# Three of eight comparisons of each head on GpSimd in the first layer of a two-layer graph attention kernel

## What is computed

```
s_src, s_dst = per node and head          # Wh . a_src, Wh . a_dst
e = s_src[:, None, :] + s_dst[None, :, :]
e = where(e >= 0, e, 0.2 * e)             # leaky relu
e = where(adj > 0, e, -9e15)
attention = softmax(e, axis=1)
h' = einsum('ijh,jhd->ihd', attention, Wh)
x1 = layernorm(x + elu(h'))
```

## Time and profile before

| what | value |
|---|---|
| median of three runs | 916.73 us (915.87 to 918.69) |
| the profiled execution | 914.89 us |
| its span, first to last instruction | 913.1 us |
| busy share of the span: PE, DVE, ACT, POOL | 92%, 83%, 76%, 5% |
| mean granted TensorE clock | 0.976 of full speed |
| chunk 0 (units with XORs from 85.5), chunks 1, 2, 3 | to 175.75, then 120.78, 119.18, 128.17 us |
| all after chunk 3 | 369.2 us |

### The profile page before, as it was taken

How to read it: one execution, slowest core, us unless ns; L and a number is a source line. 1 busy time by engine, 2 the same in 40 slices (tenths; PEclk the granted TensorE clock), 3 DMA queues, 4 the chain that set the end, 5 groups by cost and what they waited for, 6 DMA issues and landing times.

```text
span 913.1 us, 24394 instructions
## 1 busy us (share of the span) xinstructions
PE 839.0 (92%) x10868; PEld 686.8 (75%) x10868; DVE 761.4 (83%) x1306; ACT 694.4 (76%) x815; POOL 43.0 (5%) x80
## 2 busy tenths in 40 slices
PE   8496999989999889999998898599999999999995
PEld 6496999978999879999998884355555555555552
DVE  3978889899988999889997889775877786878876
ACT  3999998897999989999986994968373654637222
POOL 3200000000000000000000000000000100000000
PEclk9799999999999999999999999799999999999998
DMA  8999377703658227113040002430324453644000
GB/s 146 177 106 249 54 86 77 233 25 35 85 71 197 84 25 86 34 69 143 25 118 19 7 27 68 70 104 13 104 86 159 137 177 104 198 129 153 2 12 14
DMA packets 42065, 84.67 MB, mean 93 GB/s; under 512 B 6242, under 2 KB 31332, under 8 KB 41316
## 3 DMA queue, kind: packets, MB, share of 16 engines
q0 software_dynamic: 12416, 33.56, 26.3%
q1 hardware_dynamic: 29540, 49.50, 15.1%
HBM read 112.27 MB, written 21.12 MB: 146 GB/s over the span
## 4 chain that ended last, share of the span: by engine, by line
PE 50%; ACT 24%; DVE 18%; issue 3%; DMA 3%; POOL 1%; SPq 0%; DVEq 0%; ACTq 0%
PE bank L1299 21%; PE bank L688 18%; ACT ring L620 16%; PE bank L1277 7%; ACT masks L767 3%; DVE ring L653 3%; DVE ring L633 3%; DMA adj_tiles<-in_adj_dram 3%; PE bank L1289 2%; PE bank L536 2%; ACT masks L523 1%; DVE evac L704 1%; DVE ring L657 1%; DVE ring L663 1%; ACT moving L573 1%
## 5 line engine op out<-in xcount | busy, mean ns | idle before, releaser
L688 PE MATMUL bank<-moving,ring 128*128 128x99 bf16 (+1 forms) x6528 | 451.9, 218 | 12.2 <-DVE ring L663 8.8
L688 PEld LDWEIGHTS bank<-moving,ring 128*128 128x128 fp8e4 x6528 | 388.2, 98 | 14.3 <-DVE ring L663 10.0
L620 ACT ACTIVATE ring<-s_rows,scores 128x1024 fp8e4<-128x1024 f32 x372 | 393.1, 1141 | 4.4 <-PE bank L688 3.7
L688 PE MATMUL bank<-moving,masks 128*128 128x99 bf16 x1664 | 222.7, 209 | 18.3 <-DVE evac L704 14.7
L688 PEld LDWEIGHTS bank<-moving,masks 128*128 128x128 fp8e4 x1664 | 163.1, 98 | 20.3 <-DVE ring L657 9.1
L1299 PE MATMUL bank<-moving,masks 128*128 128x387 bf16 x1056 | 178.2, 327 | 0.0
L767 ACT ACTIVATE masks<-s_rows,adj_tiles 128x512 fp8e4<-128x512 f32 x256 | 157.8, 709 | 0.1
L1299 PEld LDWEIGHTS bank<-moving,masks 128*128 128x128 fp8e4 x1056 | 101.7, 96 | 73.0
L653 DVE SCALAR_TENSOR_TENSOR ring<-ring,masks 128x1024 int32<-128x1024 int32 x93 | 113.1, 1217 | 10.9 <-ACT ring L620 10.8
L663 DVE TENSOR_TENSOR ring<-masks,ring 128x1024 int32<-128x1024 int32 x76 | 93.1, 1225 | 26.9 <-PE bank L688 25.2
L395 ACT ACTIVATE ring<-ring 128x4 f32<-128x4 f32 (+1 forms) x24 | 4.9, 205 | 141.0 <-DVE ring L311 115.3
(11 more groups left out here) (214 smaller groups left out, 630.7 us busy)
## 6 DMA issues: line engine op xcount, KB each, us to landing
masks_kept<-masks SPq DMA_DIRECT2D x4, 4096.0 KB, 17.2
masks<-masks_kept SPq DMA_DIRECT2D x8, 2048.0 KB, 9.9
adj_tiles<-in_adj_dram POOLq DMA_DIRECT2D x24, 512.0 KB, 8.5
s_rows<-score_rows SPq DMA_DIRECT2D x14, 512.0 KB, 4.8
ring<-masks_kept POOLq DMA_DIRECT2D x11, 512.0 KB, 3.9
first_part<-masks_kept POOLq DMA_DIRECT2D x11, 512.0 KB, 3.8
second_part<-masks_kept POOLq DMA_DIRECT2D x10, 512.0 KB, 4.0
adj_tiles<-in_adj_dram POOLq DMA_DIRECT2D x16, 256.0 KB, 14.1
```

The lines of the kernel that those rows point to most:

```text
L620: last = act.activation(j_tile(below, k), s_rows[:, h % 2, :], ACT.Sign, bias=scores[:, g * JU + k, h:h + 1], saturate=False)
L688: last = pe.matmul(bank[b][:, at + lo:at + hi], mask, moving[:, j, h, lo:hi], start=first, stop=(j == T - 1), skip_group_check=True)
```

## The change

- `COMPARES` replaces `ON_ACT`, with three letters. In chunks 1 to 3 each head is `APAAPAPA`: ScalarE five units, GpSimd (P) three, VectorE none. Chunk 0 stays as it was.
- GpSimd's comparison (`pool_unit`) is four tensor_scalar instructions per unit, from f32 scores, (score + score) x -1e20, written as a byte. VectorE's AND for such a unit has a constant besides, which keeps one bit of each byte.
- The direct units of chunks 1 to 3 are 4, 4 and 8, where they were 8, 8 and 19.
- The XOR is a scalar_tensor_tensor instruction with a logical shift by zero ahead of it, where it was a tensor_tensor instruction, in all chunks.
- GpSimd's transfers of adjacency rows now stand between its comparisons, each behind unit u for the groups that TensorE turns at unit u - 4.
- SP's loads of score rows also wait for GpSimd.

```diff
-    ON_ACT = [who == "A" for who in
-              "VAVAAVAA" "AVAVAAVA" "AVAVAAVA" "AVAVAAVA"
-              "AVAAVAAA" "AVAAVAAA" "AVAAVAAA" "AVAAVAAA"
...
+    COMPARES = ("VAVAAVAA" "AVAVAAVA" "AVAVAAVA" "AVAVAAVA"
+                "APAAPAPA" "APAAPAPA" "APAAPAPA" "APAAPAPA"
...
-              "DD------" "DD------" "DD------" "DD------"
-              "DD------" "DD------" "DD------" "DD------"
-              "DD-DD-D-" "DD-DD-D-" "DD-DD-D-" "DD-D-D--"]
+              "D-------" "D-------" "D-------" "D-------"
+              "D-------" "D-------" "D-------" "D-------"
+              "D--D----" "D--D----" "D--D----" "D--D----"]
...
+        def pool_unit(pool, c, u):
+
+            h, g = divmod(u, UH)
+            if g == 0:
+                wait_s(pool, c, u)
+            if ON_POOL[c * U + u]:
+                wait_slot(pool, c, u)
+                below = below_slot(c, u).bitcast(U8)
+                for k in range(JU):
+                    last = pool.tensor_scalar(j_tile(below, k), s_rows[:, h % 2, :], scores[:, g * JU + k, h:h + 1],
+                                              FAR, ALU.add, ALU.mult)
+                last.then_inc(pool_compared, 1)
+            if g == UH - 1:
+                pool.wait_ge(pool_compared, pool_count(c, u + 1))
+                pool.sem_inc(s_read_pool, 1)
...
+            elif ON_POOL[c * U + u]:
+                dve.wait_ge(pool_compared, pool_count(c, u + 1))
+                dve.scalar_tensor_tensor(out=below, in0=below, scalar=TWO * 0x01010101, in1=m, op0=ALU.bitwise_and,
+                                         op1=ALU.bitwise_and).then_inc(done, 1)
...
-                dve.tensor_tensor(above_slot(c, u).bitcast(I32), m, below, ALU.bitwise_xor).then_inc(unit_ready, 1)
+                dve.scalar_tensor_tensor(out=above_slot(c, u).bitcast(I32), in0=below, scalar=0, in1=m,
+                                         op0=ALU.logical_shift_right, op1=ALU.bitwise_xor).then_inc(unit_ready, 1)
...
+                    if before > H:
+                        sp.wait_ge(s_read_pool, before - H)
...
                 for c in range(1, NC):
-                    for t in range(CT):
...
-                        load_adj(pool, c, t)
+                    for u in range(U):
+                        pool_unit(pool, c, u)
+                        for q in groups_at(c, u - POOL_AHEAD):
+                            t = q // QT
+                            if q % QT == QT - 1 and t + AHEAD < CT:
+                                load_next(c + 1, t + AHEAD)
+                            elif q % QT == QT - 1 and c + 2 < NC:
+                                load_next(c + 2, t + AHEAD - CT)
```

34 lines of the change are left out of this document (24 added, 10 removed).

## The result

| | before | after |
|---|---|---|
| median on the chip | 916.3 us (914.98 to 918.69) | 945.59 us (945.06 to 946.5) |
| span of the profiled execution | 913.1 us | 943.3 us |
| mean granted TensorE clock | 0.976 | 0.958 |
| chunks 1, 2, 3 | 120.78, 119.18, 128.17 us | 129.22, 129.45, 139.97 us |
| all after chunk 3 | 369.2 us | 367.9 us |

A forecast was written before the change was run, and what follows sets the result against it. PE, VectorE and ScalarE were taken as close together, VectorE setting head 0, PE and ScalarE holding each other in head 2. Terms -10.3 - 8.7 - 1.6 - 1.6 - 11.0 = -33.2 us gave 883.5 from 916.73; range 872 to 925.

The forecast's parts named there:

- free running: Chunks 1 to 3: GpSimd's comparisons run beside VectorE without holding it up; -33.2 us, to 883.5 us; chance 0.68.
- the port: Rival, chunks 1 to 3: VectorE's two-input instructions and GpSimd's comparisons take turns; 1014 us, or 927; chance 0.18.
- the 0.53 us that I set against it: GpSimd's transfer at 224.36 kept this length beside a two-input VectorE instruction; cited against shared access.
- The 0.89 us at 274.09: Length of a GpSimd transfer beside VectorE's tensor_scalar comparisons; cited as a sign that something is shared.
- a window of 9 us: Time from unit u - 6 done to u - 3 done, in which a GpSimd unit of 6 us fits without a wait.
- GpSimd's own cost: GpSimd's comparison of 1024 elements: 1.5 us taken, 0.9 to 2.24 kept; a unit 6 us, a head 18.
- -10.3 and -8.7: Chunks 1 and 2: 110.5 us each against 120.78 and 119.18, VectorE setting head 0 and PE the rest.
- the 1 us allowed for waits: Chunk 3, head 1: waits and lateness from head 0 added to VectorE's 28.0 us, giving 29.2 against 30.78.
- The walk of these heads: Chunk 3, heads 2 and 3: VectorE's work followed alone, some 46 us; 56.5 for both heads, -11.0.
- Fewer direct units: 19 units cost PE 2.92 us instead of 4.14, 23 us off PE; VectorE gets 19 XORs, 24 us.
- XOR form and transfers: Both XOR forms last 1.22 us: nothing; the transfers' wait costs GpSimd nothing, each adding only 0.53 us of work.
- the signs listed for the port: ANDs and XORs stretched to 2 us and more, or VectorE idle beside a running GpSimd.

The follow-up runs named there:

- the memset: Changed kernel with each GpSimd comparison replaced by a memset, a fill of the same bytes with zeros that reads no input: 894.41 us, ratio 0.9774.
- copy: Changed kernel with GpSimd's 144 comparisons replaced by tensor_copy, reading the same scores and writing the same bytes, without arithmetic: 949.19 us, ratio 1.0368.

## Why the prediction was wrong, point by point

**The step that failed is the question whether a comparison on GpSimd runs freely.** It took the trace's two transfers for the nearest evidence, gave free running 0.68 and the port 0.18. But the transfers only write, as the prediction said itself, and beside two-input instructions writing is the case that does not collide. A comparison that reads does not run freely: alone it takes 1.11 us, between VectorE's instructions some 3.04, and XORs of 1.22 us take up to 2.03. The Trainium skill's rule ("SBUF — State Buffer", section "Who interferes with whom": a VectorE instruction with two SBUF inputs contends with a GpSimd one that reads) holds here: the memset ran beside XORs of 1.22 us, copy and comparison stretched them to 1.9 to 2.08. Nothing in the trace stood against that rule, since no row in it had GpSimd read beside VectorE's two-input instructions, and the 0.53 us that I set against it agree with the rule. The 0.89 us at 274.09 do not follow from it: that transfer wrote beside comparisons with one input, and the run with fills shows that writing and instructions with one input can collide. The prediction's other sentence, that the second to come stands still until the first is done, does not hold for the order of turns: the AND of 253.06 went ahead of the comparison of 252.14. The chance should have been the other way round.

**The rival had the right mechanism and a wrong price.** It let VectorE's two-input instructions and GpSimd's 1.5 us take strict turns: 155 us a chunk, or 126 at 0.9 us. Measured are 129.2, 129.5 and 140.0. The comparison alone takes 1.11 us, and it holds VectorE up by 0.72 to 0.83 us. The rival's sum was a sum of work on VectorE's side; what ends last in the middle heads is GpSimd with one turn in 3.11 us, 10.9 to 11.5 for the longest units, beside a window of 9 us. It also lacked what TensorE pays for waits: 0.95 of granted clock against 0.99.

**GpSimd's own cost.** 1.5 us was taken, between 0.9 and 2.24; alone it is 1.11. The bound held, and four times 1.11 would have fitted the window as said.

**With free running, the sum was nearly right in chunks 1 and 2 and not in chunk 3.** The version that writes without reading comes nearest to that mechanism: 894.4 us, where the steps gave 883.5. Chunks 1 and 2 took 111.8 and 113.1 us against 110.5, so two of the terms, -10.3 and -8.7, were right to 1.3 and 2.6 us. Chunk 3 took 122.1 against 114. In head 1 VectorE was busy 28.0 us, exactly the sum's number, but the head took 31.4: the 1 us allowed for waits was 3.4. Heads 2 and 3 took 61.9 us against 56.5. ScalarE's wait for the late weights stayed (10.0 us), but some 3 us of it are the instructions that stood behind the fills, so these heads are no clean test of the term. The walk of these heads has a slip besides: its pieces (13 units with 2 to 3 direct ones, 3.6, and five times 2.4) add up to some 44 us, not 46.

**Fewer direct units.** The -23 us on PE and +24 on VectorE are right in kind. In the run with fills PE is busy 321 us in the three chunks, where it was 344, and with the new direct units alone VectorE is busy 22 us longer. In the sum the 61 us of comparisons that leave VectorE cover the 24, and the collisions used that cover up. Without it the step alone costs 14 us.

**XOR form and transfers.** Both at nothing. The form is 3 us of 945 at most, and not in favour of the old one; VectorE's wait for GpSimd (10.4 us) comes from GpSimd's comparisons, and its transfers take 0.55 us beside VectorE's two-input instructions.

**What would show it.** Of the signs listed for the port one came true: XORs stretched to 2 us, 56 of 95. The ANDs were hardly touched (1.23 and 1.33 us in the mean), which the prediction did not tell apart.
